# A Mamba layer with a mixture-of-experts layer behind it: shared expert spread over the next tile, with a buffer of its own; statistics behind the residuals

## What is computed

```python
# layer 1 (Mamba), di = 512, N = 16 states
h = rmsnorm(x) * norm_scale @ w_in
xs, res = split(h);  res = silu(res);  xs = silu(causal_conv4(xs) + conv_b)
delta, B, C = split(xs @ w_xproj);  delta = softplus(delta @ w_dt + b_dt)
s[t] = exp(delta[t] * A) * s[t-1] + (delta[t] * xs[t]) * B[t]      # for each of 512 x 16
y = sum_n(s * C);  out = ((y + xs * D) * res) @ w_out
x = layernorm(x + (x + out))
# layer 2 (8 experts, top 2, and a shared one), H = 1024
n = rmsnorm(x) * norm_weight
shared = relu(n @ sw1 + sb1) @ sw2 + sb2
w, e = top2(sigmoid(n @ router_w.T));  w = w / (sum(w) + 1e-6)
x = layernorm(x + shared + sum_j w_j * expert_{e_j}(n))
```

## Time and profile before

| | us |
|---|---|
| median of 3 runs | 1705.01 |
| the runs | 1704.47, 1705.01, 1710.85 |
| profiled execution, own time | 1701.9 |
| its span, first to last instruction | 1699.9 |
| PE busy in the span | 1473.8 (87%) |
| DVE busy | 1193.3 (70%) |
| ACT busy | 905.6 (53%) |
| POOL busy | 951.9 (56%) |

### The profile page before, as it was taken

One profiled execution on the slowest core, in us unless ns is written; L12 is line 12 of the kernel. 1 busy time (PEld: TensorE's weight loads), 2 busy tenths in 40 slices (PEclk: granted clock), 3 DMA queues, 4 the chain that ended last, 5 costly groups with the idle time before them and its releaser, 6 DMA issues.

```text
span 1699.9 us, 24636 instructions
## 1 busy us (share of the span) xinstructions
PE 1473.8 (87%) x6945; PEld 956.4 (56%) x6946; DVE 1193.3 (70%) x2113; ACT 905.6 (53%) x1778; POOL 951.9 (56%) x590
## 2 busy tenths in 40 slices
PE   7386799998998989989989859989999999999970
PEld 3121234534535525525525415779999999999960
DVE  4488999999999999999999999313333333333327
ACT  4477666777766777766777644223333333333324
POOL 1677797898798798898798894411111111111115
PEclk9699897998998997999998889999999999999995
DMA  5933743645545554554454440855555555555538
GB/s 155 222 99 72 165 112 75 144 115 118 135 127 114 135 128 109 137 130 120 104 133 113 115 121 7 282 171 182 185 188 193 192 191 195 195 188 185 185 132 264
DMA packets 137447, 252.14 MB, mean 148 GB/s; under 512 B 15809, under 2 KB 68914, under 8 KB 137250
## 3 DMA queue, kind: packets, MB, share of 16 engines
q1 hardware_dynamic: 130898, 233.49, 49.3%
q0 software_dynamic: 6480, 17.83, 2.8%
HBM read 205.76 MB, written 45.51 MB: 148 GB/s over the span
## 4 chain that ended last, share of the span: by engine, by line
PE 53%; DVE 27%; ACT 11%; issue 6%; DMA 1%; POOL 1%; SPq 1%; DVEq 0%; ACTq 0%; POOLq 0%
DVE psH L1127 17%; PE psH L1544 15%; PE psP L1555 14%; PE psP L1385 6%; DVE big L1136 6%; PE psP L1374 4%; PE psA L1464 3%; PE psP L1448 2%; ACT psH L963 2%; PE psA L1483 2%; PE psP L1403 2%; PE psP L1532 1%; PE psA L1474 1%; ACT L839 1%; PE psP L1420 1%
## 5 line engine op out<-in xcount | busy, mean ns | idle before, releaser
L472 POOL TENSOR_TENSOR big<-big,B 128x2048 f32<-128x2048 f32 x128 | 578.1, 4530 | 108.6 <-PE psA L1483 58.1
L963 ACT ACTIVATE psH<-big,A_q 128x512 f32<-128x512 f32 x512 | 351.8, 690 | 151.0 <-DVE big L1136 126.2
L1127 DVE TENSOR_TENSOR_SCAN psH<-psH,big 128x512 f32<-128x512 f32 x256 | 311.9, 1219 | 50.4 <-ACT psH L963 30.6
L1136 DVE TENSOR_TENSOR big<-psH,C 128x512 f32<-128x512 f32 x512 | 343.2, 670 | 0.0
L1127 DVE TENSOR_TENSOR_SCAN psH<-psH,carry,big 128x512 f32<-128x512 f32 x256 | 325.9, 1273 | 10.2 <-ACT psH L963 10.2
L576 POOL DMA_INDIRECT con_dram<-eo,dest x71 | 68.1, 960 | 470.6 <-ACT eo L1035 462.7
L1544 PEld LDWEIGHTS psH<-nTb,ew_s 128*128 128x128 f32 x2272 | 266.0, 193 | 3.6
L1544 PE MATMUL psH<-nTb,ew_s 128*128 128x128 f32 x2272 | 266.3, 276 | 0.0
L1483 PE MATMUL psA<-big,gsum 128*32 128x512 f32 x1024 | 222.2, 656 | 45.8 <-DVE big L1136 44.6
L1555 PE MATMUL psP<-big,hT 128*128 x1136 | 257.0, 379 | 0.7 <-DVE eb L1293 0.7
L1555 PEld LDWEIGHTS psP<-big,hT 128*128 128x128 f32 x1136 | 210.3, 190 | 26.7 <-issue 1.1
(11 more groups left out here) (173 smaller groups left out, 1531.5 us busy)
## 6 DMA issues: line engine op xcount, KB each, us to landing
ew_s<-in_L_ffn_ew_dram SPq DMA_DIRECT2D x71, 1024.0 KB, 4.9
big<-ud_dram SPq DMA_DIRECT2D x128, 512.0 KB, 8.5
ud_dram<-ud SPq DMA_DIRECT2D x32, 512.0 KB
xb<-rows_dram SPq DMA_DIRECT2D x71, 130.0 KB, 2.1
B<-bc_dram SPq DMA_DIRECT2D x128, 64.0 KB, 5.6
C<-bc_dram SPq DMA_DIRECT2D x128, 64.0 KB, 5.8
big<-in_L_ffn_ew_dram SPq DMA_DIRECT2D x8, 1024.0 KB
big<-con_dram SPq DMA_DIRECT2D x16, 512.0 KB, 8.7
```

What stands on the lines that cost most here:

```text
L472: nc.gpsimd.tensor_tensor(X[:, Q % NX], rep[:, g % 2, 1], B4[:, f:f + 1, :].broadcast_to([P, NR, TC]), ALU.mult).then_inc(bx_ready, 1)
L963: nc.scalar.activation(psH[:, r, :], rep[:, g % 2, 0, r, :], ACT.Exp, scale=A_q[:, c, r, f:f + 1]).then_inc(dA_ready, 1)
L1127: nc.vector.tensor_tensor_scan(psH[:, r, :], psH[:, r, :], X[:, Q % NX, r, :], start, ALU.mult, ALU.add).then_inc(scan_done, 1)
L1136: nc.vector.tensor_tensor(X[:, Q % NX, r, :], psH[:, r, :], C4[:, f, :], ALU.mult).then_inc(hc_ready, 1)
```

## The change

xnT becomes a buffer of stage 1, nT one of its own. With this I4 to I6 of the next tile move to steps 11, 13 and 14, and I7 to step 0 of its own tile. U and N are spread from steps 10 of one tile to 8 of the next but one's loop body (U7, N6, N7 at steps 6, 7, 8). ACT's parts move with them, and its share of delta's chain (`dt_exp` to `dt_less_one` of the second half) starts a group or so earlier. On DVE `stats` and `moments` follow the two residuals directly; `add_rows` moves from (3,1), (3,2) to (9,2), (9,3) and from (14,1), (14,2) to (0,1), (0,2) of the next tile. SP's stores of these rows and `load_x` move accordingly, `load_rep(k, 3)` goes ahead of them. In `LAST`, O0 and O1 come first, and N4, U6 of the last but one tile are added.

```diff
--- before.py
+++ after.py
@@ -124,8 +124,7 @@
         tail_row = sb("tail_row", [1, E], I32)
 
 
-        xnT = sb("xnT", [P, DC, TC])
-        nT = xnT
+        nT = sb("nT", [P, DC, TC])
         res = sb("res", [P, 2, CH, TC])
         w_out_s = sb("w_out_s", [P, CH, D])
         xrow = sb("xrow", [P, 2, NSUB, ROW])
@@ -190,6 +189,7 @@
 
         stage1 = ExitStack()
         sb = alloc(stage1)
+        xnT = sb("xnT", [P, DC, TC])
         w_in_s = sb("w_in_s", [P, DC, 2 * DI])
         w_xp_s = sb("w_xp_s", [P, CH, R + 2 * N])
         w_dt_s = sb("w_dt_s", [R, DI])
@@ -332,36 +332,38 @@
         block = whole.enter_context(nc.Block())
 
 
-        PE_STEPS = {0: ([("D", 2, 0)], [("D", 3, 0), ("N", 5, -2), ("U", 7, -2)]),
-                    1: ([("T", 0, 1)], [("T", 1, 1), ("N", 6, -2)]),
-                    2: ([("O", 0, -1)], [("O", 1, -1), ("N", 7, -2)]),
-                    3: ([("I", 0, 1)], [("I", 1, 1), ("I", 4, 1)]),
-                    4: ([("C", 0, 1)], [("I", 2, 1), ("I", 5, 1)]),
-                    5: ([("C", 1, 1)], [("I", 3, 1), ("I", 6, 1)]),
-                    6: ([("C", 2, 1)], [("I", 7, 1)]),
-                    7: ([("C", 3, 1)], []),
-                    8: ([], [("X", 0, 1)]),
+        PE_STEPS = {0: ([("D", 2, 0)], [("D", 3, 0), ("I", 7, 0)]),
+                    1: ([("T", 0, 1)], [("T", 1, 1), ("N", 4, -2), ("U", 6, -2)]),
+                    2: ([("O", 0, -1)], [("O", 1, -1)]),
+                    3: ([("I", 0, 1)], [("I", 1, 1), ("N", 5, -2)]),
+                    4: ([("C", 0, 1)], [("I", 2, 1)]),
+                    5: ([("C", 1, 1)], [("I", 3, 1)]),
+                    6: ([("U", 7, -2)], [("C", 2, 1)]),
+                    7: ([("N", 6, -2)], [("C", 3, 1)]),
+                    8: ([("N", 7, -2)], [("X", 0, 1)]),
                     9: ([("D", 0, 1)], [("D", 1, 1), ("R", 0, -1), ("R", 1, -1)]),
                     10: ([], [("L", 0, -1), ("U", 0, -1)]),
-                    11: ([("U", 1, -1)], [("N", 0, -1)]),
-                    12: ([("U", 2, -1)], [("N", 1, -1), ("U", 3, -1)]),
-                    13: ([("N", 2, -1)], [("U", 4, -1)]),
-                    14: ([("N", 3, -1)], [("U", 5, -1)]),
-                    15: ([], [("N", 4, -1), ("P", 0, -1), ("U", 6, -1)])}
+                    11: ([("U", 1, -1)], [("I", 4, 1)]),
+                    12: ([("U", 2, -1)], [("N", 0, -1)]),
+                    13: ([("N", 1, -1)], [("U", 3, -1), ("I", 5, 1)]),
+                    14: ([("N", 2, -1)], [("U", 4, -1), ("I", 6, 1)]),
+                    15: ([("U", 5, -1)], [("N", 3, -1), ("P", 0, -1)])}
 
 
         PE_FIRST = [("T", 0), ("T", 1), ("I", 0), ("I", 1), ("C", 0), ("I", 2), ("C", 1), ("I", 3), ("C", 2), ("C", 3),
                     ("X", 0), ("D", 0), ("D", 1)]
 
-        LAST = ([("N", 5, NT - 2), ("O", 0, NT - 1), ("O", 1, NT - 1), ("U", 7, NT - 2), ("N", 6, NT - 2), ("N", 7, NT - 2)] +
-                [(use, i, NT - 1) for use, i in [("R", 0), ("R", 1), ("L", 0), ("U", 0), ("U", 1), ("N", 0), ("P", 0)]] +
+        LAST = ([("O", 0, NT - 1), ("O", 1, NT - 1)] +
+                [(use, i, NT - 2) for use, i in [("N", 4), ("U", 6), ("N", 5), ("U", 7)]] +
+                [("R", 0, NT - 1), ("R", 1, NT - 1), ("L", 0, NT - 1), ("N", 6, NT - 2), ("N", 7, NT - 2)] +
+                [(use, i, NT - 1) for use, i in [("U", 0), ("U", 1), ("N", 0), ("P", 0)]] +
                 [(use, i + d, NT - 1) for i in range(1, 7) for use, d in (("U", 1), ("N", 0))] + [("N", 7, NT - 1)])
 
         def pe_step(k, n):
 
             parts = tuple([(use, i, k + d) for use, i, d in part if 0 <= k + d < NT] for part in PE_STEPS[n])
             if k == 0 and n == 0:
-                parts[1].extend([("I", CH, 0), ("I", CH + 1, 0)])
+                parts = (parts[0], [("D", 3, 0), ("I", CH, 0), ("I", CH + 1, 0)])
             if k == 0 and n == 1:
                 parts = ([("I", CH + 2, 0)], [("I", CH + 3, 0)] + parts[0] + parts[1])
             if k >= NT:
@@ -680,13 +682,15 @@
                     load_rep(k, 1)
                 if k + 2 < NT:
                     load_xr(k + 2)
+                if k >= 2:
+                    store_acc(k - 2, 0)
                 store_ud(k, 2)
+                load_rep(k, 2)
+                store_ud(k, 3)
+                load_rep(k, 3)
                 if k >= 2:
                     store_acc(k - 2, 1)
-                load_rep(k, 2)
-                store_ud(k, 3)
                 load_x(k)
-                load_rep(k, 3)
                 if k + 1 < NT:
                     store_bc(k + 1)
                     load_b(k + 1, 0)
@@ -699,12 +703,11 @@
                     load_c(k + 1, 1)
                     load_b(k + 1, 3)
                     load_c(k + 1, 2)
-                if k:
-                    store_acc(k - 1, 0)
                 if k + 1 < NT:
                     load_c(k + 1, 3)
 
 
+            store_acc(NT - 2, 0)
             sp.wait_ge(y_acc, NT * NQ)
             for e in range(E):
                 sp.dma_start(ew2_s[:, e], ew2[e].rearrange("(c p) n -> p c n", p=P)).then_inc(s_w3, 16)
@@ -918,30 +921,34 @@
                         ins.then_inc(relu_done, 1)
                 ins.then_inc(p_free[bank_of(k, ("U", i))], 1)
 
-            ACT_STEPS = {(0, 2): [(dt_in, 0, 2)], (0, 3): [(relu_up, -2, 6)],
-                         (1, 0): [(dt_in, 0, 3)], (1, 2): [(relu_up, -2, 7)],
-                         (2, 0): [(read_rows, 1, 0), (dt_exp, 0, 1)], (2, 1): [(read_rows, 1, 1), (dt_ln, 0, 1)],
-                         (2, 2): [(dt_one_plus, 0, 1)], (2, 3): [(dt_less_one, 0, 1)],
-                         (3, 1): [(silu_gate, 0)],
-                         (4, 0): [(read_in, 1, 0)], (4, 2): [(read_in, 1, 1)], (4, 3): [(read_in, 1, 4)],
-                         (5, 1): [(read_conv, 1, 0)], (5, 2): [(read_in, 1, 2)], (5, 3): [(read_in, 1, 5)],
-                         (6, 1): [(read_conv, 1, 1)], (6, 2): [(read_in, 1, 3)], (6, 3): [(read_in, 1, 6)],
-                         (7, 1): [(read_conv, 1, 2)], (7, 2): [(read_in, 1, 7)],
+            ACT_STEPS = {(0, 0): [(relu_up, -2, 5)], (0, 2): [(read_slots, -2)], (0, 3): [(dt_in, 0, 2)],
+                         (1, 1): [(dt_in, 0, 3)], (1, 2): [(read_in, 0, 7)], (1, 3): [(dt_exp, 0, 1)],
+                         (2, 0): [(read_rows, 1, 0), (dt_ln, 0, 1)], (2, 1): [(read_rows, 1, 1), (dt_one_plus, 0, 1)],
+                         (2, 2): [(dt_less_one, 0, 1)], (2, 3): [(relu_up, -2, 6)], (3, 1): [(silu_gate, 0)],
+                         (4, 0): [(read_in, 1, 0)], (4, 2): [(read_in, 1, 1)],
+                         (5, 1): [(read_conv, 1, 0)], (5, 2): [(read_in, 1, 2)],
+                         (6, 1): [(read_conv, 1, 1)], (6, 2): [(read_in, 1, 3)],
+                         (7, 0): [(relu_up, -2, 7)], (7, 2): [(read_conv, 1, 2)],
                          (8, 0): [(read_conv, 1, 3)], (8, 1): [(silu_xs, 1)],
                          (9, 1): [(normalize, -1, 0)], (9, 2): [(read_proj, 1)], (9, 3): [(normalize, -1, 1)],
                          (10, 0): [(dt_in, 1, 0)], (10, 1): [(dt_in, 1, 1)],
                          (10, 2): [(read_nT, -1, 0)], (10, 3): [(read_nT, -1, 1)],
                          (11, 0): [(dt_exp, 1, 0)], (11, 1): [(read_logits, -1), (dt_ln, 1, 0)],
-                         (11, 2): [(one_more, -1), (dt_one_plus, 1, 0)], (11, 3): [(dt_less_one, 1, 0), (relu_up, -1, 0)],
-                         (12, 0): [(relu_up, -1, 1)], (13, 0): [(relu_up, -1, 2)], (13, 2): [(relu_up, -1, 3)],
-                         (0, 1): [(read_slots, -2)], (14, 2): [(relu_up, -1, 4)],
-                         (15, 0): [(norm_row, 2, 0)], (15, 1): [(norm_row, 2, 1)],
-                         (15, 2): [(norm_row, 2, 2), (relu_up, -1, 5)], (15, 3): [(norm_row, 2, 3)]}
-            GATES_0 = {(1, 1): [(read_in, 0, 4)], (1, 2): [(read_in, 0, 5)], (1, 3): [(read_in, 0, 6)],
-                       (2, 0): [(read_in, 0, 7)]}
+                         (11, 2): [(one_more, -1), (dt_one_plus, 1, 0)],
+                         (11, 3): [(dt_less_one, 1, 0), (relu_up, -1, 0)],
+                         (12, 0): [(relu_up, -1, 1)], (12, 2): [(read_in, 1, 4)], (12, 3): [(norm_row, 2, 0)],
+                         (13, 0): [(relu_up, -1, 2)], (13, 2): [(norm_row, 2, 1)],
+                         (14, 0): [(relu_up, -1, 3)], (14, 2): [(read_in, 1, 5)], (14, 3): [(norm_row, 2, 2)],
+                         (15, 0): [(relu_up, -1, 4)], (15, 2): [(read_in, 1, 6)], (15, 3): [(norm_row, 2, 3)]}
+            GATES_0 = {(1, 1): [(read_in, 0, 4)], (1, 2): [(read_in, 0, 5)], (1, 3): [(read_in, 0, 6)]}
+            GATES_1 = {(2, 0): [(read_in, 0, 7)]}
 
             def parts(k, at):
-                for part, d, *which in (GATES_0.get(at, []) if k == 0 else []) + ACT_STEPS.get(at, []):
+                steps = ACT_STEPS.get(at, [])
+                if k == 0:
+                    steps = [step for step in steps if step != (read_in, 0, 7)]
```

(18 more changed lines are left out.)

## The result

The median of seven runs is **1696.7 us** against 1705.0 before: ratio 0.9943 [0.9929, 0.9957]. Measured once more it was 1692.1, 0.9929 [0.9916, 0.9941]. So the change is worth 0.6 to 0.7%, 10 to 12 us by the ratios, where 3.2 were forecast. The profiled execution took 1698.1 of its own, 3.8 less than the profiled one of before.

A forecast was written before the change was run, and what follows sets the result against it. The loop goes at DVE's pace, with some 42 us of idle time to win. Terms -10.4 + 6.6 - 3.65 - 0.7 + 1.5 - 1.0 - 0.9 + 5.3 = -3.2 gave a median of 1701.8 us, range 1691 to 1714.

The forecast's parts named there:

- a few us less: Whole kernel: the forecast itself, -3.2 us to a median of 1701.8, chance 0.48.
- signs of being wrong: Residual waiting over 2 us, silu later by over 0.5, tail below 67, or DVE's loop idle time outside 25 to 40.
- Step 1: Scan waits in step 1 of tiles 2 to 7: all vanish, as ACT no longer waits for PE there, -10.4 us.
- Step 2: DVE's residual in step 2 newly waits for O0: 0.2 to 2.0 a tile, 1.1 taken for six tiles, +6.6 us.
- B: Rival, slower: PE at half clock from T0 to O0, residual 3.8 late in six tiles, 1718 us, chance 0.14.
- Step 3: Even tiles' waits of 1.2 in step 3: moved statistics cover ACT's table loads, -3.65 us for three tiles.
- Step 8: C3 behind `add_state` and N6 ends 0.3 later, silu with it: +1.5 us in five tiles; no gain valued.
- Tile 0: Step 8 of tile 0, which has no U and N: C3 comes earlier, -1 us.
- Steps 10 to 12: Waits of 3 us noted in the loop's steps 10 to 12; no change priced for them.
- Tail: Behind the loop: R later +1.8, N6 and N7 between router and U0 +3.5, together +5.3 us, bounds +1.9 to +8.9.
- Zero terms: I4 to I6 at steps 11 to 14, SP's queue and the separate buffer: each claimed to cost nothing.
- the small waits of step 2: Small waits of 0.24 in step 2 of the loop: claimed to go, -0.7 us.

The follow-up runs named there:

- 3: Kernel before with only the relu of U7 one group later on ACT, at (1,3) instead of (1,2): ratio 0.9956 to the kernel before.
- 4: Changed kernel with DVE's statistics back at (3,3) to (4,2): ratio 0.9955 to the kernel before.
- Experiment 7: Changed kernel with C3 ahead of `add_state` and N6 in step 7: ratio 0.9842 to the kernel before.
- 8: Changed kernel with ACT's `normalize` of the last tile ahead of the last U7's relu, in the tail: ratio 0.9889 to the kernel before.
- experiment 9: Changed kernel with SP's store of the last shared rows' first half behind the eight writes of zeros: ratio 0.9916 to the kernel before.
- experiment 5: Kernel before with statistics directly behind the residuals and `add_rows` later, at (4,0) and (4,1): ratio 1.0040 to the kernel before.

## Why the prediction was right, and where it was not

The time, 1696.7, is within the range and 5 below the forecast; the case that held, a few us less, ends just past the half percent where I had put it just short. Two of my signs of being wrong came all the same: a residual waited over 2 us (3.48 in tile 7), and the table load of the silu in step 8 came 1.0 later in the odd tiles, measured from the step's first scan (0.8 behind it, before 0.2 ahead). By its steps:

- **Step 1.** The mechanism is right (3 shows it). Its size was mis-measured: 10.4 is one execution's; another had 13.8. All of it went. I took a wait that depends on the clock from a single execution that was itself 3 us under its median, and carried the 3 over as if it belonged to something else; the execution with 13.8 took 1706.6. Against the medians this is the largest single error of the sum.
- **Step 2.** Forecast 6.6, measured 5.1 and 5.8. But not 1.1 in each of six tiles: 0.7 to 0.8 in two or three of them and 3.5 in the last, where the low clock lasted 10.2. That the sum came near is luck. "The low clock of step 1 lasted some 3.5 us", my argument against B, was a misreading already: that holds for tiles 2, 4 and 5 of the kernel before, and in tiles 3, 6 and 7 it lasted 6.8. B's own sum also puts its bound at 3.05 a tile, not 2.8 (-9.8 and six times 3.05 make 8.5). Windows of tiles 3 and 7 of the kernel before, the clock 0.50 throughout:

```profile
444.00:450.00 6.00, 5.99 (x11) 3.69 (x12) 5.44 (x8) 3.00 (x5) 4.65 (x6) 0.50 1.06 234
...
946.00:952.00 6.00, 6.00 (x14) 3.88 (x13) 5.52 (x7) 2.46 (x4) 3.86 (x6) 0.50 1.08 216
```

- **Step 3.** The waits went, as forecast (1.2 in three tiles), the reason was wrong: 4 has none either. ACT comes to the silu 2 us or more sooner. That delta's last part of the second half (`dt_less_one`) stands a group earlier than before could explain it, and so could the relu of U7 that no longer holds ACT up, since 3 halves the wait by itself; on the changed kernel neither was tried apart. The statistics' own share is at most the 4 us of experiment 4, through residuals.
- **Step 8.** The term was mis-sized: +0.3 in each, measured +0.1 to +0.2 in even tiles and +1.0 in odd ones, tile 1 without an N6 among them (+3.5 in all for +1.5). I priced the end of C3 by the products ahead of it and not the place itself: C3, the last thing ahead of ACT's block, stood behind `add_state`, which can't end before DVE's last product of the step. Experiment 7 shows this place to cost 13 us of waits, more than the whole change won. I had written "I value no gain there" and did not ask what is possible there.
- **Tile 0.** Forecast -1 in step 8, measured -0.5; steps 1 to 3, which I left out, went from 5.5 to 7.0.
- **Steps 10 to 12.** 3.3 went to 1.5, not forecast. Fewer U and N stand there; that this is the cause was not tried.
- **Tail.** +5.3 forecast, +6.1 measured. R is 1.7 later, as said. Router, N6 and N7 cost 6.8 instead of 3.5, since they now have the low clock, and U0, U1, which no longer have it, give 2.4 back; 8 confirms the relu ahead of `normalize`.
- **Zero terms.** I4 to I6, SP's queue and the buffer cost nothing; no wait of DVE on a B, C or x load came up.

Sum of what changed in the two profiles: -10.4 (step 1) + 5.1 (step 2) - 3.6 (step 3) + 3.5 (8) - 0.5 + 1.6 (tile 0) - 1.8 (10 to 12) - 1.4 (the small waits of step 2, and one of step 7 in tile 0) - 1.0 (a gate that waited in tile 0) - 2.2 (DVE's busy time) = -10.7, of the 10.9 that the loop gave; with the other execution's step 1 it is -14.1. With the tail's 6.1 and the experts' 0.9 the profiled executions differ by 3.8, which is near the 3.2 of my sum; the second pair of them differs by 10.0, the medians by 8.3 and 12.8. The forecast was right about one pair of executions and low about the kernels. Even for that pair it is in part luck: step 8, tile 0, the tail and the experts came out some 6 us dearer than forecast, and what I had too high or at nothing (step 2, steps 10 to 12, the small waits, the gate, DVE's busy time) some 6 us cheaper.

Of the clock in step 1 of the changed kernel, first profile: PE's gap is 2.02 in tiles 2, 4 and 6, 1.85 in tiles 3 and 5, and 2.71 in tile 7, which has no T. The clock stayed at 1.00 in tiles 2, 3 and 5, whose residual did not wait; it fell to 0.50 for 3.4 us in tiles 4 and 6 (waits of 0.80 and 0.81; N4 itself, behind that stretch in tile 4, took its 1.99), and for 10.2 us in tile 7 (3.48). The Trainium skill ("TensorE: Matmul & The Clock Gate", Part 1) says that the throttled clock is the default state and that activity releases it. That alone does not tell the tiles apart: behind the same 2.02 the trace has 0.50 in tiles 4 and 6 and 1.00 in tile 2, where the second profile has 0.50 too.

## What to carry to other kernels

In a loop whose engines run fixed streams in order, ask of every part who waits for it next, and do not put it behind a part that must itself wait for another engine: C3 moved ahead of `add_state` was worth 15 us and one relu moved by a group 7, where the restructuring with its new buffer gave 10. Look for a tile in which the suspected part is missing: tile 1, without N6, tells it from `add_state`. A wait that hangs on PE's clock differs between executions of the same program, so read a second execution before it is priced, and before an experiment's difference of 1 or 2 us is believed. A wait taken away at one place need not shorten the time (experiment 5).

## What was not expected of the hardware

The granted clock behind the same gap is not the same from tile to tile and from profile to profile, nor does it fall for the same time: 3.4 us in tiles 4 and 6, 10.2 us in tile 7, where N4 took 3.78 (eight records of 128x256, 1.99 at full clock). Behind the same 2.71 in tile 7 it fell in both profiles of the changed kernel and not in that of experiment 9. In the tail, the router (sixteen records of 128x8) took 3.55 us behind PE's waits of 3.07 and 0.87, and 2.35 where the first of them was gone. The eight writes of zeros took 11.8 and 12.0 in two executions of one program, and 13.0 with the store behind them.
